# Cross attention and routed FFN: the output bias goes into the value table, small norm steps change engines, and the softmax exponential is done head by head

## The reference, cut to what matters

```python
# x (4, 1024, 512), context (4, 64, 512), 16 heads of 64, all float32
q, k, v = heads(layernorm(x) @ Wq.T), heads(context @ Wk.T), heads(context @ Wv.T)
sim = einsum('bhid,bhjd->bhij', q, k) * 64 ** -0.5
sim = where(masks, sim, -max_float)
attn = softmax(sim)                                   # over the 64 keys of a head
x = x + einsum('bhij,bhjd->bhid', attn, v).merged @ Wo.T + bo
z = layernorm(x)
expert = argmax(softmax(z @ gate_w.T))                # one of 2 for each row
x = x + relu(z @ w1[expert] + b1[expert]) @ w2[expert] + b2[expert] \
      + b2[other] + relu(b1[other]) @ w2[other]       # the other expert sees a row of zeros
      + relu(z @ sw1 + sb1) @ sw2 + sb2               # shared net, hidden 2048
```

## Time and profile before

| | |
|---|---|
| median of 3 runs | 1966.02 us (1962.3 to 1966.55) |
| the profiled execution's own time | 1961.06 us |
| its span, first to last instruction | 1959.3 us |
| mean granted TensorE clock | 0.986 of full |
| TensorE busy | 1856.2 us, 95% of the span |
| VectorE busy | 851.8 us, 43% |
| ScalarE busy | 835.5 us, 43% |
| GpSimd busy | 526.1 us, 27% |
| DMA | 206.00 MB, 105 GB/s in the mean |

### The profile page before, as it was taken

The page is one execution under the profiler, slowest core; times in us unless marked ns, Lnnn a source line. Parts: engine busy times, 40 slices in busy tenths (PEclk is TensorE's granted clock), DMA queues, the critical chain, the costliest instruction groups (busy, mean ns, idle before and its releaser), DMA issues. The chain is left out here.

```text
span 1959.3 us, 34126 instructions
## 1 busy us (share of the span) xinstructions
PE 1856.2 (95%) x11704; PEld 1170.5 (60%) x11705; DVE 851.8 (43%) x1571; ACT 835.5 (43%) x1473; POOL 526.1 (27%) x635
## 2 busy tenths in 40 slices
PE   8889989999779999999999999899999999999997
PEld 6344444444346666666666666566666666666664
DVE  6978778777624433444333333322222222222222
ACT  4654544455323333334544544333343333343333
POOL 1057777777600000100000100211212211212211
PEclk9999999999979999999999999999999999999998
DMA  9234433433382232223344465731121111121200
GB/s 319 76 90 121 125 118 120 131 112 108 108 283 76 76 102 82 97 87 106 118 145 144 140 225 184 240 84 44 49 61 48 55 43 40 47 60 46 62 23 15
DMA packets 186855, 206.00 MB, mean 105 GB/s; under 512 B 87568, under 2 KB 129040, under 8 KB 186384
## 3 DMA queue, kind: packets, MB, share of 16 engines
q1 hardware_dynamic: 178848, 179.66, 29.7%
q0 software_dynamic: 7920, 25.17, 4.1%
HBM read 129.56 MB, written 58.98 MB: 96 GB/s over the span
## 5 line engine op out<-in xcount | busy, mean ns | idle before, releaser
L975 PE MATMUL pH<-room_a,room_w 128*128 128x256 f16 (+1 forms) x6336 | 770.2, 272 | 11.7 <-DMA room_w<-s_split 8.7
L987 PE MATMUL pY<-room_w,room_a 128*128 128x512 f16 (+1 forms) x3120 | 756.7, 380 | 12.8 <-DVE room_a L1006 12.8
L975 PEld LDWEIGHTS pH<-room_a,room_w 128*128 (+1 forms) x6336 | 614.1, 98 | 192.6 <-issue 11.8
L1006 DVE TENSOR_TENSOR room_a<-room_a 128x256 f16<-128x256 f32 (+1 forms) x528 | 233.7, 443 | 911.6 <-ACT room_a L1000 909.3
L987 PEld LDWEIGHTS pY<-room_w,room_a 128*128 128x128 f16 x3120 | 305.6, 98 | 277.4 <-DVE room_a L1006 13.4
L998 ACT ACTIVATE room_a<-pH,e_bsel,sc 128x256 f32<-128x256 f32 (+1 forms) x272 | 152.0, 559 | 433.3 <-PE pH L975 408.3
L998 ACT ACTIVATE room_a<-pH,b1s,sc 128x256 f32<-128x256 f32 x256 | 144.4, 564 | 395.6 <-PE pH L975 395.6
L1172 POOL TENSOR_TENSOR room_a<-room_a,s_brow 128x512 f32<-128x512 f32 x32 | 42.4, 1348 | 600.9 <-DVE room_a L1014 600.9
L464 PE MATMUL pO<-room_w,room_b 128*128 (+1 forms) x768 | 174.3, 384 | 7.1 <-DVE room_b L690 7.1
L1000 ACT ACTIVATE room_a<-pH,e_bsel,sc 128x256 f16<-128x256 f32 (+1 forms) x272 | 149.7, 550 | 0.0
L1000 ACT ACTIVATE room_a<-pH,b1s,sc 128x256 f16<-128x256 f32 x256 | 142.4, 556 | 0.0
(11 more groups left out here) (182 smaller groups left out, 1476.9 us busy)
## 6 DMA issues: line engine op xcount, KB each, us to landing
s_er<-in_w SPq DMA_DIRECT2D x64, 512.0 KB, 5.1
room_w<-e_split SPq DMA_DIRECT2D x8, 2048.0 KB, 17.9
rows_room<-in_x SPq DMA_DIRECT2D x32, 256.0 KB, 2.7
room_a<-in_sw SPq DMA_DIRECT2D x32, 256.0 KB, 3.1
room_b<-in_x SPq DMA_DIRECT2D x32, 256.0 KB, 2.8
s_split<-room_a SPq DMA_DIRECT2D x64, 128.0 KB, 2.7
x_scratch<-room_b SPq DMA_DIRECT2D x32, 256.0 KB, 3.0
z_split<-room_b SPq DMA_DIRECT2D x32, 256.0 KB, 2.0
```

Source lines behind the costliest of these rows:

```text
L975: mm = q.matmul(self.pH[j % 2][:, 0:rows], w[:, k, j * P:(j + 1) * P], zt[:, u, k, 0:rows], start=(n == 0), stop=(n == 3 * KC - 1))
L987: mm = q.matmul(self.pY[u][r][:, :], h[:, j % self.HR, r * P:(r + 1) * P], w[:, j, :], start=(j == 0 and n == 0), stop=(j == HC - 1 and n ...
L1006: q.tensor_tensor(self.hl[:, j % self.HR, 0:rows], self.hf[:, j % self.HR, 0:rows], self.hh[:, j % self.HR, 0:rows], ALU.subtract).then_in ...
```

## The change

- **Bias folded.** bo is loaded (as `bob`) behind Wo in the tables stage. For the first pair of heads of each batch one more float32 matmul adds it to the first head's rows of the value table: since the probabilities of a head add up to 1, the output has bo in it. The scale of the table takes its largest value in. `add_bo` is gone, and `residual` waits for the load of its row itself.
- **Norm scalars.** GpSimd keeps only the power of -0.5 of each norm (`deviation`, `deviation2`). Adding the epsilon (`add_eps`, `add_eps2`) and making the shifts (`shifts`, `shifts2`) go to VectorE, the latter behind `gate`. `lo_z` goes from VectorE to the end of GpSimd's list, for tile i-1.
- **Exponential.** `sub` is gone. VectorE makes minus the maxima (`mxn`) behind L743, and ScalarE does 16 exponentials of 128 x 64 for each tile, one for each head, with that head's column of `mxn` as bias, in place of one of 128 x 1024.
- **Loads.** `load_next` is called at the start of iteration 31 instead of its end, and loads all four quarters of the shared net's weights. The shared net's block begins with `load_e(0)`.

```diff
                 sp.dma_start(wo_v, ...).then_inc(in_wo, 16)
+                sp.dma_start(bob, bo.partition_broadcast(P)).then_inc(in_bo, 16)
...
         def body(g):                                   # SyncE, attention
             for u in range(N):
+                if last_tile(g, u):
+                    load_next()
                 ...
                 step(sp, g, u, -2, store_z)
-                if last_tile(g, u):
-                    load_next()
         def load_next():
             ...
             sp.wait_ge(S["sim"], SUB)
-            load_quarter(sp, wA, s1_d, s2_d, 0, 1, first_in["w1_in0"])
-            load_quarter(sp, wA, s1_d, s2_d, 0, 2, first_in["w2_in0"])
+            for q in range(QUARTERS):
+                load_quarter(sp, wA, s1_d, s2_d, q, 1, first_in[f"w1_in{q}"])
+                load_quarter(sp, wA, s1_d, s2_d, q, 2, first_in[f"w2_in{q}"])
...
                 mm = pe.matmul(pk[n % 4], vd[:, q, b, :, :]..., wo_v[:, q, :], start=True, stop=(q > 0))
+                if q == 0:
+                    mm = pe.matmul(pk[n % 4], head0, bob, start=False, stop=True)
...
         def exp(e, g, u):                              # ScalarE
             e.wait_ge(S["sub"], count(g, u))
-            e.activation(s[:, u % 2, :, :], s[:, u % 2, :, :], ACT.Exp).then_inc(S["exp"], 1)
+            for h in range(HEADS):
+                v = e.activation(s[:, u % 2, h, :], s[:, u % 2, h, :], ACT.Exp, bias=mxn[:, u % 2, h:h + 1])
+            v.then_inc(S["exp"], 1)
...
         def body(g):                                   # GpSimd
             for u in range(N):
                 step(pool, g, u, 2, negate)
-                step(pool, g, u, 4, rs_1)
-                step(pool, g, u, -1, rs_2)
+                step(pool, g, u, 4, deviation)
+                step(pool, g, u, -1, deviation2)
                 step(pool, g, u, 1, norm)
                 step(pool, g, u, 3, lo_x)
-                step(pool, g, u, 0, add_bo)
-                step(pool, g, u, 2, sub)
                 step(pool, g, u, 2, low_w)
+                step(pool, g, u, -1, lo_z)
...
+        def deviation(e, g, u):
+            e.wait_ge(S["ve"], count(g, u))
+            e.tensor_tensor(rs[:, u % 2, :], ve[:, u % 2, :], half[:, :], ALU.pow).then_inc(S["rs_x"], 1)
...
+        def add_eps(e, g, u):                          # VectorE
+            e.wait_ge(S["agg"], count(g, u))
+            e.tensor_scalar(ve[:, u % 2, :], mv[:, u % 2, 1:2], EPS, None, ALU.add).then_inc(S["ve"], 1)
+        def shifts(e, g, u):
+            e.wait_ge(S["rs_x"], count(g, u))
+            e.scalar_tensor_tensor(out=shift1[:, u % 2, :], in0=mv[:, u % 2, 0:1], scalar=-1.0, in1=rs[:, u % 2, :],
+                                   op0=ALU.mult, op1=ALU.mult).then_inc(S["rs"], 1)
+        def shifts2(e, g, u):
+            e.wait_ge(S["rs_z"], count(g, u))
+            e.tensor_scalar(rs2[:, u % 2, :], rsz[:, u % 2, :], LN_SCALE, None, ALU.mult)
+            e.scalar_tensor_tensor(out=shift2[:, u % 2, :], in0=mv2[:, u % 2, 0:1], scalar=-LN_SCALE, in1=rsz[:, u % 2, :],
+                                   op0=ALU.mult, op1=ALU.mult).then_inc(S["rs2"], 1)
...
             e.tensor_reduce(mx[:, u % 2, :], s[:, u % 2, :, :], AX.X, ALU.max).then_inc(S["mx"], 1)
+            e.wait_ge(S["mx"], count(g, u))
+            e.tensor_scalar(mxn[:, u % 2, :], mx[:, u % 2, :], -1.0, None, ALU.mult).then_inc(S["sub"], 1)
...
                 step(dve, g, u, 4, aggregate)
                 step(dve, g, u, -1, aggregate2)
+                step(dve, g, u, 4, add_eps)
+                step(dve, g, u, -1, add_eps2)
                 step(dve, g, u, 2, masked)
                 step(dve, g, u, -1, agg2_done)
                 step(dve, g, u, -1, gate)
+                step(dve, g, u, 4, shifts)
+                step(dve, g, u, -1, shifts2)
                 step(dve, g, u, -1, pick)
-                step(dve, g, u, -2, lo_z)
...
-    for q in range(1, Q):                              # SyncE, shared net
-        load_quarter(sp, wA, s1_d, s2_d, q, 1, S[f"w1_in{q}"])
-        load_quarter(sp, wA, s1_d, s2_d, q, 2, S[f"w2_in{q}"])
+    load_e(0)
     sp.dma_start(brow[:, :], sb2.partition_broadcast(P)).then_inc(S["brow_in"], 16)
     ...
     load_r(0)
-    load_e(0)
```

More of the change, by code:

```diff
@@ L188, in xattn_ffn @@
         wB = weight_set(room_v)
-        first_in = {n: sem("s_" + n) for n in ("w1_in0", "w2_in0")}
+        first_in = {n: sem("s_" + n) for q in range(QUARTERS) for n in (f"w1_in{q}", f"w2_in{q}")}
         snet = Net("s", TILES, sem, sc, ident, A1, A2, room_a, rows_room, banks_a)
@@ L270, in xattn_ffn @@
                 mx = take([2, HEADS])
+                mxn = take([2, HEADS])
                 sm = take([2, HEADS])
@@ L286, in xattn_ffn @@
                 mv2 = sb("mv2", [P, 2, 2], F32, a)
+                rs2 = sb("rs2", [P, 2, 1], F32, a)
+                rsz = sb("rsz", [P, 2, 1], F32, a)
+                ve = sb("ve", [P, 2, 1], F32, a)
                 ve2 = sb("ve2", [P, 2, 1], F32, a)
[L288 to L291, removed]
+                half = sb("half", [P, 1], F32, a)
                 shift1 = sb("shift1", [P, 2, 1], F32, a)
@@ L613, in _ @@
                         pool.partition_all_reduce(amr[:, 2:4], am[:, 2:4], P, RMAX).then_inc(reduced, 1)
-                        pool.wait_ge(S["half_set"], 2)
-                        def rstd(src_sem, mv, ve, minus_m, rs, shift, ves, made_rs, used, done, gain=None):
-                            def fn(e, g, u):
-                                e.wait_ge(src_sem, count(g, u))
-                                if gain is not None:
-                                    e.tensor_tensor(minus_m[:, u % 2, :], mv[:, u % 2, 0:1], minus[:, :], ALU.mult)
-                                    e.tensor_scalar(ve[:, u % 2, :], mv[:, u % 2, 1:2], EPS, gain ** -2, ALU.add, ALU.mult).then_inc(ves, 1)
-                                else:
-                                    e.tensor_tensor(ve[:, u % 2, :], mv[:, u % 2, 1:2], eps[:, :], ALU.add)
-                                    e.tensor_tensor(minus_m[:, u % 2, :], mv[:, u % 2, 0:1], minus[:, :], ALU.mult).then_inc(ves, 1)
-                                e.wait_ge(ves, count(g, u))
-                                at_least(e, used, count(g, u) - 2)
-                                e.tensor_tensor(rs[:, u % 2, :], ve[:, u % 2, :], half[:, :], ALU.pow).then_inc(made_rs, 1)
-                                e.wait_ge(made_rs, count(g, u))
-                                e.tensor_tensor(shift[:, u % 2, :], minus_m[:, u % 2, :], rs[:, u % 2, :], ALU.mult).then_inc(done, 1)
-                            return fn
@@ L639, in norm, with deviation2 @@
+                        def deviation2(e, g, u):
+                            e.wait_ge(S["ve2"], count(g, u))
+                            at_least(e, S["pick1"], count(g, u) - 2)
+                            e.tensor_tensor(rsz[:, u % 2, :], ve2[:, u % 2, :], half[:, :], ALU.pow).then_inc(S["rs_z"], 1)
                         def norm(e, g, u):
@@ L655, in negate, with lo_z @@
                             e.tensor_tensor(neg[:, u % 2, :], drop[:, u % 2, :], least, ALU.mult).then_inc(S["neg"], 1)
+                        def lo_z(e, g, u):
+                            e.wait_ge(S["zh"], count(g, u))
+                            e.tensor_tensor(zs[:, u % 2, DM:2 * DM], zf[:, u % 2, :], zs[:, u % 2, 0:DM], ALU.subtract).then_inc(S["z"], 1)
                         def low_w(e, g, u):
@@ L717, in residual @@
                             e.wait_ge(S["att"], count(g, u))
-                            e.wait_ge(S["xr_bo"], count(g, u))
+                            e.wait_ge(S["r_in", u % 2], dma_count2(g, u))
                             if not isinstance(g, int) or N * g + u >= 2:
@@ L839, in _ @@
                                 aggregate(dve, 0, 0)
+                                add_eps(dve, 0, 0)
+                                shifts(dve, 0, 0)
                         def other_scales():
@@ L1130, in store_e @@
                         sp.dma_start(net.rows(units(d[1]), n), el[:, i, :, :]).then_inc(S["e_out"], 16)
[L1132 to L1136 removed]
+                load_e(0)
+                sp.dma_start(brow[:, :], sb2.partition_broadcast(P)).then_inc(S["brow_in"], 16)
                 for u in range(2):
```

74 lines of the change are left out of this document (37 added, 37 removed).

## The result

| | before | after |
|---|---|---|
| median of 4 runs | 1964.61 us (1962.3 to 1966.55) | 2002.4 us (2001.62 to 2004.89) |
| ratio, 95% interval | | 1.020 (1.0186 to 1.0213) |
| span of the profiled execution | 1959.3 us | 2000.5 us |
| mean granted clock | 0.986 | 0.981 |

The kernel became 2% slower. Its span grew by 41.2 us, and three rows of TensorE in the trace of after say where. They answer to the `t_p` rows and to the first matmul of the shared net.

The account below looks back on a forecast made before the run. A loop through three engines, not TensorE's peak, was taken to bound attention, at 13.03 us a tile. Loop +38.1, tables +3.5, fill +1.3 and passage 0 gave +42.9 us, so 2009 us, range 1990 to 2038.

Parts of the forecast that it names:

- the loop: Attention: from hi_p through exponentials, VectorE's list and normal2 back to hi_p, 14.34 us a tile, +38.1 us over 29 tiles.
- the start: Everything before the first t_p: tables +3.5 us and filling the pipeline +1.3, together +4.8.
- the passage: From t_p(29) to the shared net's first matmul, 54.6 us instead of 42.9; with the gain behind it, counted as 0.
- The exponential: ScalarE in attention: 16 activations a tile, 331 ns each, 0.25 us apart, 4.1 us in all against 1.06.
- Tables: Tables stage: four more products, bo's maximum and a wait for GpSimd's power, +3.5 us, bounds 0 and 6.
- The fill: Filling the pipeline before t_p(0): mxn and the exponentials 4.3 us instead of sub and exp, +1.3 us.
- The gain behind it: Shared net: the wait of 8.27 us for weights and the half clock behind it go, -11.1 us.
- The clock rival: TensorE in attention: sim's pause of 2.4 us a tile, where 0.6 before, lowers the clock; to 2038 us, chance 0.25.
- The hidden exponentials (E of 2.6): Attention: exponentials take 2.6 us, so the loop through sim, 13.65 us, sets the period; 1989 us, chance 0.08.
- E of 5.4: ScalarE in attention: the 16 exponentials don't overlap and take 5.4 us, loop 15.64 us; 2047 us, chance 0.05.
- The faster case: Attention: the loops don't close and TensorE's own 12.1 us a tile bounds; 1944 us, chance 0.08.
- the second: Attention: the loop through sim with its full 5.35 us and no exponential in it, 13.65 us a tile.

Follow-up runs that it names:

- a_norm_waits: a_shift_first plus one wait: GpSimd's norm of tile i+1 waits for VectorE's second shift of tile i-1; 1954.6 us, ratio 0.9961.
- a_norms_back: The changed kernel with the norm scalars back on GpSimd as before, lo_z staying on GpSimd; 1963.1 us, ratio 1.000.
- a_shift_first: The changed kernel with VectorE doing gate, shifts and shifts2 ahead of masked instead of behind it; 1989.0 us, ratio 1.0133.
- a_head0_late: The changed kernel with the bias row's two memsets and their wait moved behind GpSimd's first all-reduce; 1995.3 us, ratio 1.0169.
- a_split_loads: The changed kernel with two of the four weight quarters loaded behind the stores of tile 29; 1991.8 us, ratio 1.0144.
- a_exp_one: The changed kernel with one exponential for all 16 heads, no bias and no subtraction of the maximum; 1975.8 us, ratio 1.0068.

## Why the prediction came out as it did

**Total.** 2009 was given, 2002.4 measured, inside the range of 1990 to 2038 and in the forecast's own range of 2000 to 2018. That the total is so close is luck in part: the loop was 16.2 us too high, the start 10.0 too low and the passage 4.4 too low, which leaves 1.8 of error in a sum of 42.9. The other 5.0 us are the median of before, to which the sum was added, against its profiled execution.

**The loop: mechanism right, size too large.** Forecast 14.34, measured 13.73. Step by step, forecast and measured: `hi_p` 0.93 and 0.90; exponentials with handover 4.2 and 4.06; `sums`, aggregates and `add_eps` 1.93 and 1.78; `masked`, maxima and `mxn` 2.62 and 2.92; `gate` 0.91 and 0.67; shifts with handover 0.65 and 0.31; `normal2` to `hi_p` 3.10 and 3.09. The mis-sized terms are the small steps on VectorE: I took 0.2 each from `pick`, but `pick` is 0.21 to its end, and such steps in a row start 0.06 to 0.08 apart. `gate` had been read to the start of `pick`, which waits for it; the shifts don't. Against that `mxn` took 0.43 beside `norm`, and 0.17 elsewhere. By this one iteration they are 0.61 x 29 = 17.7 us; the mean period is 0.05 longer than it, which leaves the 16 us.

**The exponential: right.** 331 ns each, 0.25 apart and 4.1 in all were forecast; 342 ns, 0.24 apart and 3.93 in all were measured. The fits over the rows of other shapes carried. The Trainium skill, "ScalarE: Activation LUTs", section "What ACT_TABLE_LOAD costs", gives an estimate of 3.9 us by its figures; the trace agrees with 3.93.

**What the loop contains: only partly seen.** The forecast named the shift behind `masked` and `gate` as the point, and a_norm_waits and a_norms_back bear it out. It didn't name what shares the blame: GpSimd's `norm` beside VectorE's shift, `gate` or `mxn`.

**Tables: wrong.** +3.5 was forecast with 6 as the upper bound; the first `t_p` shows that tables and fill cost 14.8 in place of 4.8, of which the tables have 10.8, outside the bound. The step that failed is "four more are 3.8 us, minus what fits in 2.2 us of idle time, plus bo's maximum": it prices the added products and doesn't ask what the memsets of `head0`, which the changed kernel has on GpSimd ahead of the all-reduce, stand in front of. The products were worth 2.2, in the bounds. The fill was +4.05 instead of +1.3: from the end of the last product to `t_p`(0) it is 23.71 us (113.97 to 137.68), before 19.66. Of this the exponentials' start is 2.2 late: `mxn` ended at 127.19, but ScalarE's list had `normal` and two steps of `scale_w` in front, and they began at 129.38.

**Passage: shape right, sum 4 short.** Forecast 54.6 us from `t_p`(29) to the net, measured 58.6. The weights started at 22.7 (560.10) instead of 20 and took 20.3 (to 577.55 + 2.88) instead of 23. From their end to `residual`(31), with the store of z in it, it was 8.7 where I had estimated 3, and from there to the net 6.9 instead of 8.65: 2.7 - 2.7 + 5.7 - 1.7 = +4.0. The gain behind it was 11.3, against the 11.1 forecast, and the wait of 8.27 us is gone.

**Rivals.** The clock rival happened in single tiles only. As a rule `sim` waited some 2 us and took 5.35, at a granted clock of 0.99 over the stage; in tile 12 it waited 1.98 and took 7.04, which made this tile and the next together 0.9 us longer than the same pair four tiles on (28.64 against 27.72). Tile 0 was slow too (0.83), behind a pause of 5.77 us. So nearly the same pause was followed by the full clock in most tiles and by the half in one, and no run shows what decides it. a_shift_first had two such tiles behind its first, a_head0_late and a_split_loads three, before none; each puts some 0.03 us on the period in the table, an estimate from tile 12. Behind the pause of 6.33 us before 48.78 four matmuls took twice their time, and in the weights' gap the clock fell to 0.54. The hidden exponentials (E of 2.6) and E of 5.4 fell with the 3.93. The faster case needed both loops below 13.03; measured, the first was 13.73, and by a_exp_one the second stood at 13.02.

## What to carry to other kernels

When a pipelined kernel runs at the length of a loop through several engines, ask for each moved step what stands ahead of it in its new list: here 0.3 us of scalars behind 2.9 us of other work (and behind the sums that wait for ScalarE) cost some 39 us, and putting them ahead, with one wait for order, gave 48. Price what a new instruction delays, not what it takes: two memsets of 0.35 us in front of an all-reduce cost 9 us, and stores behind sixteen weight loads cost 11. And where a tiny instruction takes 1.8 us in the trace, look at what runs beside it before its own cost is believed.

## What the hardware showed that I had not expected

- **VectorE beside GpSimd.** Some VectorE instructions were held while a GpSimd instruction ran beside them. The shift (128 x 1) took 1.78 in place of 0.15 us and ended with `norm`; `gate` took 2.41 in place of 0.74 and `lo_z` 2.32 in place of 0.68, both ending 0.55 after `norm`, as if most of their work came behind it. It goes the other way too: GpSimd's power took 1.07 beside `gate`, 0.55 otherwise. These three VectorE instructions read two operands from SBUF. `masked`, which reads PSUM and SBUF, ran beside `norm` both in after and in a_norm_waits and took 1.28; the maxima, which read one operand from SBUF, took their 1.22 beside it. But `mxn`, which reads one too, was held: 0.43 in place of 0.17 at 397.22, and more at the start of after:

```profile
137.59 1.15 POOL L641 TENSOR_TENSOR room_a<-room_a 128x512 f16<-128x512 f32 x1
137.64 1.13 DVE L760 TENSOR_SCALAR room_b<-room_b 128x16 f32<-128x16 f32 x1
```

  The trace of before had the sign in it, and the prediction passed over it: `lo_z` 1901 ns in the mean. The Trainium skill, "GPSIMD Engine Reference", section "1. Specifications", says that GpSimd shares its SBUF interfaces with VectorE, with contention where VectorE's instruction has two SBUF inputs or is in a 2-port perf mode. The rows of the shift, `gate` and `lo_z` agree with the first; whether `mxn` ran in such a mode no run shows. That the shared interface is the cause was tested only by moving instructions apart, not by taking operands elsewhere.
- **GpSimd before its first all-reduce.** 6.42 us passed between the memset and the all-reduce, with nothing waited for. The second all-reduce of after started at 79.42, 0.10 us after its maxima, so the gap didn't come again. In a_head0_late and before the gap isn't seen; there GpSimd waited 28 us for the maxima, and the time may have passed in that wait. What GpSimd does in it, the trace doesn't show.
